# Embed stage stores unit rows instead of x1, VectorE takes over the up bias, Gram-Schmidt steps move one place

## What is computed

```python
hidden = gelu(einsum('bsd,ad->bsa', x, down_W) + down_b)
hidden = hidden @ Wsel.T + bsel + domain_emb[idx]        # expert chosen per batch
x0 = layernorm(hidden @ up_W.T + up_b + x) * gamma + beta
```

```python
unit = _ln(x0)
x1 = unit * (1.0 + scale) + shift                        # scale, shift per batch
q, k, v = x1 @ Wq + bq, x1 @ Wk + bk, x1 @ Wv + bv
probs = softmax(where(mask, -inf, q @ k.T / sqrt(32) + attention_bias))   # 16 heads
x2 = x1 + (probs @ v) @ Wo + bo
h = _ln(x2) * g2 + beta2
x2 = x2 + gelu2(h @ W1 + b1) @ W2 + b2
```

```python
for i in range(32):
    q = Q[:, i] / (norm(Q[:, i]) + EPS)
    Q[:, i+1:] -= outer(q, q @ Q[:, i+1:])
```

## Time and profile before

| | us |
|---|---|
| median of three runs | 3844.51 (3843.71 to 3854.38) |
| the profiled execution | 3847.99 |
| its span, first to last instruction | 3846.0 |
| TensorE busy | 3645.8 (95%) |
| VectorE, ScalarE, GpSimd busy | 2357.8, 2170.6, 2174.4 |

### The profile page before, as it was taken

The page is one execution under the profiler, slowest core; times in us unless marked ns, Lnnn a source line. Parts: engine busy times, 40 slices in busy tenths (PEclk is TensorE's granted clock), DMA queues, the critical chain, the costliest instruction groups (busy, mean ns, idle before and its releaser), DMA issues. The chain is left out here.

```text
span 3846.0 us, 79741 instructions
## 1 busy us (share of the span) xinstructions
PE 3645.8 (95%) x31793; PEld 2479.6 (64%) x31793; DVE 2357.8 (61%) x4491; ACT 2170.6 (56%) x3002; POOL 2174.4 (57%) x739
## 2 busy tenths in 40 slices
PE   4988988999999999999999999997899999999997
PEld 2444436888888888888888788886444444444443
DVE  6777656888888888888888788884212111212112
ACT  1333336999989999889999899995111111011100
POOL 2243317998889899889998799994212011111100
PEclk8999998999999999999999999998999999999995
DMA  3444449999999999999999999996100010000005
GB/s 112 169 165 169 175 182 363 327 324 323 323 373 333 323 324 324 351 337 327 325 324 335 349 329 324 325 326 251 43 23 22 23 33 12 22 33 12 11 1 195
DMA packets 210153, 830.89 MB, mean 216 GB/s; under 512 B 24034, under 2 KB 57954, under 8 KB 134532
## 3 DMA queue, kind: packets, MB, share of 16 engines
q1 hardware_dynamic: 205444, 817.53, 61.5%
q10 hardware_dynamic: 4352, 8.39, 0.6%
HBM read 733.04 MB, written 92.80 MB: 215 GB/s over the span
## 5 line engine op out<-in xcount | busy, mean ns | idle before, releaser
L1072 POOL TENSOR_TENSOR at_tiles<-at_tiles,at_negmask 128x1792 f32<-128x1792 f32 x512 | 1837.9, 3633 | 274.1 <-DMA at_tiles<-in_bias 207.5
L1162 ACT ACTIVATE at_tiles<-at_tiles,at_rmin 128x2048 f32<-128x2048 f32 x512 | 1025.2, 2002 | 75.9 <-DVE at_rmin L1209 75.9
L1108 PE MATMUL at_ps_p<-consts,at_tiles 128*128 128x128 f32 x8192 | 1025.8, 272 | 0.1
L1108 PEld LDWEIGHTS at_ps_p<-consts,at_tiles 128*128 128x128 f32 x8192 | 931.7, 142 | 36.5 <-ACT at_prob_t L1170 0.4
L1170 ACT ACTIVATE at_prob_t<-at_ps_p 128x512 f32<-128x512 f32 x1536 | 831.5, 597 | 149.9 <-PE at_ps_p L1108 149.6
L1209 DVE CUSTOM_DVE_ANT_0 at_tiles<-at_ps_s,at_tiles 128x1024 f32<-128x1024 f32 x512 | 624.6, 1220 | 157.5 <-PE at_ps_s L1089 116.7
L1089 PE MATMUL at_ps_s<-at_k_stack,at_q_stack 128*128 128x512 f32 x2048 | 680.5, 433 | 35.5 <-DMA at_q_stack<-q_lo 15.4
L1209 DVE CUSTOM_DVE_ANT_0 at_tiles<-at_ps_s,at_tiles,at_rmin 128x1024 f32<-128x1024 f32 x512 | 657.4, 1284 | 18.3
L1125 PE MATMUL at_ps_c<-at_prob_t,at_v 128*32 128x128 f32 x16384 | 502.2, 275 | 4.1 <-DMA at_v<-v 3.5
L1125 PEld LDWEIGHTS at_ps_c<-at_prob_t,at_v 128*32 128x32 f32 x16384 | 432.8, 110 | 47.8 <-issue 43.2
L1403 PE MATMUL ff_ps_m<-ff_norm_t,ff_w 128*128 128x512 f32 x1024 | 442.2, 592 | 0.8 <-ACT ff_feats L1499 0.8
(11 more groups left out here) (178 smaller groups left out, 2931.0 us busy)
## 6 DMA issues: line engine op xcount, KB each, us to landing
at_tiles<-in_bias SPq DMA_DIRECT2D x512, 1024.0 KB, 10.7
at_k_stack<-k_hi SPq DMA_DIRECT2D x128, 256.0 KB, 7.2
at_k_stack<-k_lo SPq DMA_DIRECT2D x128, 256.0 KB, 9.1
negm<-em_mask_out SPq DMA_DIRECT2D x32, 512.0 KB, 7.2
at_q_stack<-q_hi SPq DMA_DIRECT2D x128, 128.0 KB, 7.8
at_q_stack<-q_lo SPq DMA_DIRECT2D x128, 128.0 KB, 8.9
at_negmask<-negm SPq DMA_DIRECT2D x32, 512.0 KB, 15.1
at_v<-v SPq DMA_DIRECT2D x64, 256.0 KB, 11.3
```

What stands on the lines that cost most here:

```text
L1072: pool.tensor_tensor(tiles[:, s, 0:PCOLS], tiles[:, s, 0:PCOLS], negm[:, s, 0:PCOLS], ALU.add).then_inc(s_pool, 1)
L1108: last = pe.transpose(ps_p[k][:, y * P:(y + 1) * P], tiles[:, s, t * P:(t + 1) * P], ident)
L1162: act.activation(tiles[:, s, :], tiles[:, s, :], ACT.Exp, bias=rmin[:, s, 1:2], scale=-1.0, accum_out=rsum[:, s:s + 1]).then_inc(s_exp, 1)
```

## The change

In the embed stage, GpSimd no longer multiplies by scale and adds shift: the unit rows themselves are stored (`net.unit` in place of `net.x1`), from two buffers `rows_of` that alternate by tile and replace `res` and `x1`. The up bias is added by VectorE in four operations of 128x512 that stand between the V groups. In the written order, `gs_dots(r, 1)` moves ahead of projection 4, `gs_squares(r, 1)` to just behind split 3, `gs_project(r, 1)` to behind split 4, and `take_v(p, 0)` and `take_v(p, 1)` change places with neighbours. On ScalarE `take_qk(p, 7)` comes ahead of `unit_rows`. On GpSimd the second norms come ahead of the second root. In the feed-forward stage GpSimd adds `bo` to both rows of shift once, multiplies x1 by scale in four operations and adds the sum of shift and `bo` in four more, and VectorE waits for each quarter. The hardware loops of that stage are written out.

```diff
@@ embed stage, SyncE
-                    sp.wait_ge(s_xup, r + 1)
+                    sp.wait_ge(s_xup, 4 * r + 4)
...
-                    sp.wait_ge(s_x1, r + 1)
-                    sp.dma_start(x1v[r], x1[:]).then_inc(s_x1_st, 16)
+                    sp.wait_ge(s_u, 4 * r + 4)
+                    sp.dma_start(uv[r], rows_of[r % 2][:]).then_inc(s_u_st[r % 2], 16)
@@ embed stage, TensorE
                 if back:
                     project(p, 3)
+                if front:
+                    gs_dots(r, 1)
+                if back:
                     project(p, 4)
...
                     project(p, 5)
-                if front:
-                    gs_dots(r, 1)
@@ embed stage, ScalarE
+                if back:
+                    take_qk(p, 7)
                 if front:
                     unit_rows(r)
                 if back:
-                    take_qk(p, 7)
                     mask(p, 2)
@@ embed stage, GpSimd
-            add_up_bias(0)
             for r in range(NT):
-                b = batch_of(r)
                 gs_norms(r, 0)
                 root(r, 0)
+                gs_norms(r, 1)
                 root(r, 1)
-                gs_norms(r, 1)
-                if r + 1 < NT:
-                    add_up_bias(r + 1)
                 gs_norms(r, 2)
-                pool.wait_ge(s_u, 4 * r + 4)
-                after(pool, s_x1_st, 16 * r)
-                pool.tensor_tensor(x1[:], res[:], net.ada_scale[:, b, :].unsqueeze(1).broadcast_to([P, TJ, D]),
-                                   ALU.mult).then_inc(s_x1m, 1)
                 gs_norms(r, 3)
-                pool.wait_ge(s_x1m, r + 1)
-                pool.tensor_tensor(x1[:], x1[:], net.ada_shift[:, b, :].unsqueeze(1).broadcast_to([P, TJ, D]),
-                                   ALU.add).then_inc(s_x1, 1)
@@ embed stage, VectorE
+            def add_up_bias(n, parts):
+                for j in parts:
+                    dve.wait_ge(s_x, 16 * (n + 1))
+                    v.tensor_tensor(x_up[:, j, :], x_in[:, j, :], up_b[:], ALU.add).then_inc(s_xup, 1)
...
                 if back:
                     split(p, 3)
                 if front:
+                    gs_squares(r, 1)
                     centred(r, 2)
...
                     affine(r, 2)
+                if back:
+                    split(p, 4)
+                if front:
+                    gs_project(r, 1)
                     row_stats(r, 1, 1)
...
                 if front:
                     gs_squares(r, 3)
+                if r + 1 < NT:
+                    add_up_bias(r + 1, range(TJ))
                 if back:
                     take_v(p, 2)
@@ feed-forward stage
-            rounds(eng, NT + 1, batch_of, 3, NT - 2, emit)
+            for n in range(NT + 2):
+                emit(n, n, batch_of(n))
...
+            for i in range(B):
+                step(pool.tensor_tensor(net.ada_shift[:, i, :], net.ada_shift[:, i, :], bo[:], ALU.add))
...
-                    pool.tensor_tensor(x1[:], x1[:], bo[:].unsqueeze(1).broadcast_to([P, TJ, D]),
-                                       ALU.add).then_inc(s_x1b, 1)
+                    bf = n // NB
+                    for j in range(TJ):
+                        pool.tensor_tensor(x1[:, j, :], x1[:, j, :], net.ada_scale[:, bf, :], ALU.mult).then_inc(s_x1m, 1)
+                    for j in range(TJ):
+                        pool.wait_ge(s_x1m, 4 * n + j + 1)
+                        pool.tensor_tensor(x1[:, j, :], x1[:, j, :], net.ada_shift[:, bf, :], ALU.add).then_inc(s_x1b, 1)
...
-                    dve.wait_ge(s_x1b, n + 1)
...
                     for j in range(TJ):
+                        dve.wait_ge(s_x1b, 4 * n + j + 1)
                         dve.wait_ge(s_wo, 4 * n + j + 1)
```

More of the change, by code:

```diff
@@ L80, in rows @@
     return ap.rearrange("(a n) -> a n", a=1).broadcast_to([n, ap.shape[0]])
-def rounds(eng, last, batch_of, first_full, last_full, emit):
-    n = 0
-    while n <= last:
-        end = n
-        while first_full <= n and end + 1 <= last_full and batch_of(end + 1) == batch_of(n):
-            end += 1
-        if end > n:
-            with eng.Fori(n, end + 1) as i:
-                emit(i, n, batch_of(n))
-        else:
-            emit(n, n, batch_of(n))
-        n = end + 1
 class Chain:
@@ L342, in embed_stage @@
         hid2 = sb("em_hid2", [P, TOK])
-        res = sb("em_res", [P, TJ, D])
-        x1 = sb("em_x1", [P, TJ, D])
+        rows_of = [sb(f"em_rows{i}", [P, TJ, D]) for i in range(2)]
         x1_t = [sb(f"em_x1_t{i}", [P, DC, TOK]) for i in range(2)]
@@ L404, in embed_stage @@
         s_split_link = sem("em_split_steps")
-        s_x1_st = sem("em_x1_stored")
+        s_u_st = [sem(f"em_unit_rows_stored{i}") for i in range(2)]
         s_qk_st = [sem(f"em_{a}_stored") for a in "qk"]
@@ L604, in _ @@
                     project(p, 5)
-                if front:
-                    gs_dots(r, 1)
-                else:
+                if not front:
                     gs_end(3)
@@ L853, in _ @@
             gs_products(gs[0], first)
+            add_up_bias(0, range(TJ))
             for r in range(NT + 1):
@@ L900, in _ @@
                     moments(r, 1, row_stats(r, 1, 3))
-                if back:
-                    split(p, 4)
-                if front:
-                    gs_squares(r, 1)
                 else:
                     take_end(2)
-                if front:
-                    minus_mean(r)
                 if back:
@@ L911, in _ @@
                 if front:
-                    gs_project(r, 1)
+                    minus_mean(r)
                 else:
@@ L916, in _ @@
                     split(p, 6)
-                if front:
-                    gs_squares(r, 2)
-                else:
+                if not front:
                     take_end(4)
@@ L923, in _ @@
                 if front:
+                    gs_squares(r, 2)
+                if back:
+                    take_v(p, 0)
+                if front:
                     gs_project(r, 2)
                 if back:
-                    take_v(p, 0)
                     take_v(p, 1)
```

39 lines of the change are left out of this document (17 added, 22 removed).

## The result

The changed kernel takes 3788.51 us (median of four runs, 3781.57 to 3789.44), the kernel before in the same job 3844.11 us. The ratio is 0.9845, with a 95% interval of 0.9825 to 0.9866.

What follows compares the result with a forecast made beforehand. TensorE, busy 95% of the span, was taken as the bound, with waits to win in the embed stage. Gains of 42 + 3 + 8 = 53 us, taken as 52, bring 3844.5 to 3793 us, range 3783 to 3813.

Steps and rivals of the forecast that it cites:

- the likeliest case: Whole kernel: the author's own forecast of 3793 us, given 58%, with its own range of 3787 to 3799.
- GpSimd's hold: Embed stage: without GpSimd's three 128x2048 operations nothing long holds VectorE, 4 us less in the chain to the third dots.
- The order: Embed stage: earlier gs_project(r, 1) gives partial dots at +32.8; the 6.1 us wait and 1.9 us of low clock go.
- some 4 us: Embed stage, TensorE's wait at the third dots: the part put down to GpSimd's long operation; 2 to gs_project(r, 1)'s place.
- The new wait: Embed stage: TensorE waits 1.4 us at the transposes of x for ScalarE; the next round starts at +54.7.
- Four adds: Embed stage: up bias on VectorE takes 2.7 us a round where it waited for V group 2, with 4.0 us of cover.
- Stored rows, loops: Embed stage stores unit rows in place of x1, feed-forward loops are written out: no gain from the first, cost 0 for the second.
- Feed-forward: Feed-forward stage: GpSimd's eight 128x512 operations take 10.2 us, with 20 us of cover, 4.9 in round 0; cost 0.
- The unknown: Embed stage: whether the clock falls behind the 1.4 us wait; no fall taken, the other end costs 10 us.
- the rival of a low clock: Embed stage: the clock falls behind the 1.4 us wait in six rounds, 1.7 us each, total 3803; chance 20%.
- the sum of 53: Embed stage gain: 42 us from rounds 1 to 6, 3 from round 7, 8 from round 0; 52 taken.
- allowed 1.4 us for it: Embed stage: two GpSimd norm operations blocked behind VectorE's adds of 0.68 us each, inside the 4.0 us of cover.

Runs made afterwards that it cites:

- the version with the late GpSimd add: Changed kernel with the up bias added by GpSimd again, as one 128x2048 operation behind the fourth norms of the round: 3792.60 us, ratio 0.9822.

## Why the prediction held, step by step

The forecast was 3793 us, the time 3788.5, inside the range of 3783 to 3813 and inside the likeliest case's own (3787 to 3799).

1. *GpSimd's hold.* Right: 4.12 us became 0.16. The runs with the bias back on GpSimd show it in both directions: held when the operation stands beside minus_mean, harmless for the stage beside V group 2's wait. By the Trainium skill (SBUF — State Buffer, section "SBUF: two separate sides") the engine that starts first has the shared ports for its whole instruction, when VectorE's operation has two inputs in SBUF and GpSimd's reads SBUF. The trace agrees: with 0.06 us of head start for GpSimd's add, minus_mean took 4.47 us instead of 0.16.
2. *The order.* Right to a tenth: partial dots at +32.8, as said. What the prediction didn't say is that the order is worth nothing without step 1. Its sum of "some 4 us" and "2" reads as if the two could be had apart. The first can (56.90 us), the second can't (63.30).
3. *The new wait.* 1.4 us forecast, 1.20 measured, round 54.7 and 54.72. The cause, two masks ahead of the chunks, is shown by the run without them there.
4. *Four adds.* 2.7 us forecast, 2.49 measured; their cover, 5.0 us with the idle time, measured by its end.
5. and 7. *Stored rows, loops.* No wait on TensorE's list in the embed stage ends at a store, and the loops alone gave no change; that unit rows cost the same as x1 was not tried apart.
6. *Feed-forward.* In round 2 the adds end at 2793.3, 21 us ahead of need; in round 0 the fourth use starts 18.0 us behind the stage's first matmul, 17.9 before. The first use there did wait for GpSimd and came 1.3 us later than before (9.0 instead of 7.7), which the fourth, as said, does not feel.

*The unknown.* The clock held behind 1.2 us, as taken, but the reason given for it does not carry. At 2.2 us TensorE also works right up to the wait and after it, and three of six rounds paid 1.7 us. What the runs support is the length: 1.7 us was still free in six rounds of six. The row of 2.13 us, on which the rival of a low clock stood, was one of two outcomes of that wait.

*Sizes that were off.* Round 0 gave 9.0 us in the stage where I had 8, rounds 1 to 6 gave 42.9 where I had 42, round 7 gave 3.1 as said (3), and I then took 52 for the sum of 53. Another 0.7 us each came ahead of the stage's first matmul and behind round 7. The cost of low clock behind a wait of 6 us is 61.87 - 53.34 - 6.08 = 2.45 us with the restart, not 1.9: that was read in round 3, where the eight passes took 5.51 us, and it leaves out the dots themselves (0.69 instead of 0.33). All these are small. The remaining 3.2 us between the profiled spans are attention's. The prediction had it unchanged and named a change of its length as a sign of being wrong; this part of the gain was luck, and without it the time would still lie in the range. In fourteen profiles with the same attention code it lasted 2083.1 to 2094.1 us, and two executions of the changed kernel with 2086.4 and 2086.8 still differ from the 2090.8 of the version with the late GpSimd add. What sets it stays open.

## What to carry to other kernels

Before an order is changed, list what lies on VectorE beside each long GpSimd operation: the same 4.5 us add cost 6.5 us a round behind the second root and nothing in the stage 10 us later in the round. A small operation that waits for GpSimd's result is a bad neighbour of a long one that GpSimd starts next, since both become ready at the same moment; here the long one came first by 0.06 us each time that it was read, and the small one stood on the path to TensorE. I missed this neighbour in two expectations, and in the third had it only as the second choice. When a stall of several us is removed, look for the engine that stood idle because of it; its order was free until then, and here the masks moved behind what TensorE waits for gave another 1.4 us a round.

## What the runs showed of the hardware that I had not expected

- A VectorE operation with one SBUF input and one SBUF output (128x512, 0.42 us when free) was held as well, 1.49 us beside four short GpSimd operations; another of the same form was not.
- Blocking goes both ways. The prediction had allowed 1.4 us for it; it is 0.8. GpSimd's norms on 128x2 take 1.07 and 0.62 us beside VectorE's four adds. They take 0.70 and 0.19 earlier in the same round, and 0.69 and 0.20 at this very place in the version with the late GpSimd add, where VectorE has no adds:

```profile
236.69 0.70 POOL L701 TENSOR_TENSOR em_gs_norms<-em_gs_norms,em_half 128x2 f32<-128x2 f32 x1 [2.47 <-DVE em_gs_norms L732]
237.47 0.19 POOL L702 TENSOR_TENSOR em_gs_norms<-em_gs_norms,em_gs_eps 128x2 f32<-128x2 f32 x1
243.12 1.07 POOL L701 TENSOR_TENSOR em_gs_norms<-em_gs_norms,em_half 128x2 f32<-128x2 f32 x1 [5.46 <-DVE em_gs_norms L732]
244.28 0.62 POOL L702 TENSOR_TENSOR em_gs_norms<-em_gs_norms,em_gs_eps 128x2 f32<-128x2 f32 x1
```

- Equal waits of TensorE had unequal prices: 2.24 us cost nothing more in one round and 1.7 us of low clock in the next.
